# A cross-attention kernel: the first weight chunk in two transfers, six warming rounds, and four early reads of a few bytes

## The reference

```
q = x @ Wq + bq                      # 512 -> 512
k = ctx @ Wk + bk                    # 256 -> 512
v = ctx @ Wv + bv                    # 256 -> 512
w = softmax((q @ k^T) / sqrt(512), axis=tokens)   # over the 100 tokens, not over the context
y = w @ v + x
out = (y - mean(y)) * rsqrt(var(y) + 1e-6) * gamma + beta
```

## Time and profile before

| | |
|---|---|
| time, median of 3 executions | 142.33 us (142.27 to 143.05) |
| time of the profiled execution | 142.47 us |
| its span, first instruction to last | 140.7 us |
| busy: TensorE, VectorE, ScalarE, GpSimd | 134.4, 115.1, 79.7, 60.8 us |
| mean granted TensorE clock | 0.992 |

### The profile page before, as it was taken

How to read it: one execution, slowest core, us unless ns; L and a number is a source line. 1 busy time by engine, 2 the same in 40 slices (tenths; PEclk the granted TensorE clock), 3 DMA queues, 4 the chain that set the end, 5 groups by cost and what they waited for, 6 DMA issues and landing times.

```text
span 140.7 us, 2977 instructions
## 1 busy us (share of the span) xinstructions
PE 134.4 (96%) x1046; PEld 130.0 (92%) x1046; DVE 115.1 (82%) x224; ACT 79.7 (57%) x283; POOL 60.8 (43%) x61
## 2 busy tenths in 40 slices
PE   7999999999999999999999999999999999999940
PEld 7899999999998999999999999999999999998940
DVE  0689995996996779999999976878799976797983
ACT  4267098667276925567473829474746546386420
POOL 1000000037304581733839370629475643629791
PEclk9999999999999999999999999999999999999996
DMA  4999999985187595986978789697987987536314
GB/s 139 328 404 420 424 278 389 302 285 199 20 261 269 175 374 166 366 328 198 349 289 301 285 305 370 234 330 224 301 278 280 342 260 256 209 108 221 121 73 150
DMA packets 10814, 37.33 MB, mean 265 GB/s; under 512 B 1200, under 2 KB 1456, under 8 KB 10800
## 3 DMA queue, kind: packets, MB, share of 16 engines
q1 hardware_dynamic: 9424, 34.79, 71.6%
q10 hardware_dynamic: 1376, 2.36, 4.4%
HBM read 33.87 MB, written 3.28 MB: 264 GB/s over the span
## 4 chain that ended last, share of the span: by engine, by line
PE 89%; POOL 5%; issue 2%; ACT 1%; POOLq 0%; DVE 0%; DVEq 0%
PE ps_S L424 29%; PE ps_U L438 26%; PE ps_Y L459 10%; PE ps_U L397 6%; PE ps_Y L397 6%; POOL xT_in L979 3%; PE ps_Y L340 2%; POOL xT_in L967 2%; PE ps_S L345 1%; PE ps_w L447 1%; PE ps_U L504 1%; PE ps_c L412 1%; PE ps_S L351 1%; PE ps_U L351 1%; ACT xT_in L601 1%
## 5 line engine op out<-in xcount | busy, mean ns | idle before, releaser
L583 ACT ACTIVATE expo<-scores,negmax 121x100 f32<-121x100 f32 x96 | 35.0, 365 | 31.0 <-DVE negmax L754 30.9
L424 PE MATMUL ps_S<-G,ctxT_in 128*121 128x100 f32 (+1 forms) x384 | 43.4, 269 | 0.0
L424 PEld LDWEIGHTS ps_S<-G,ctxT_in 128*121 128x121 f32 (+1 forms) x384 | 42.1, 185 | 0.0
L438 PEld LDWEIGHTS ps_U<-prob,ctx_in 121*128 121x128 f32 x336 | 39.4, 192 | 0.9
L438 PE MATMUL ps_U<-prob,ctx_in 121*128 121x100 f32 x336 | 39.6, 274 | 0.0
L956 POOL TENSOR_TENSOR prob<-expo,rinv 121x600 f32<-121x600 f32 x16 | 19.2, 1202 | 30.4 <-DVE rinv L761 30.2
L967 POOL TENSOR_TENSOR xT_in<-x_in,xT_in 128x512 f32<-128x512 f32 (+1 forms) x13 | 17.1, 1315 | 19.8 <-issue 8.9
L750 DVE TENSOR_TENSOR scores<-ps_S,c_rows 121x600 f32<-121x600 f32 x16 | 12.5, 782 | 10.1 <-PE ps_S L424 7.4
L765 DVE TENSOR_REDUCE probsum<-prob 121x100 f32<-121x600 f32 x16 | 19.8, 1239 | 1.0 <-POOL prob L956 0.7
L583 ACT ACTIVATION_READ_ACCUMULATOR expo<-scores,negmax 121x1 f32 x96 | 17.9, 187 | 0.0
L972 POOL TENSOR_TENSOR rstd<-vareps,neg_half 128x1 f32<-128x1 f32 (+1 forms) x13 | 7.1, 549 | 23.3 <-DVE vareps L792 23.1
(11 more groups left out here) (120 smaller groups left out, 184.4 us busy)
## 6 DMA issues: line engine op xcount, KB each, us to landing
ctx_in<-ctx SPq DMA_DIRECT2D x16, 768.0 KB, 5.2
ctxT_in<-ctxT SPq DMA_DIRECT2D x16, 722.0 KB, 5.1
xT_in<-xT SPq DMA_DIRECT2D x8, 400.0 KB, 8.6
x_in<-x SPq DMA_DIRECT2D x12, 256.0 KB, 4.5
out<-xT_in ACTq DMA_DIRECT2D x8, 256.0 KB, 4.1
wqk<-Wqk SPq DMA_DIRECT2D x4, 388.0 KB, 4.6
out<-xT_in SPq DMA_DIRECT2D x3, 256.0 KB, 2.0
wv_in<-Wv SPq DMA_DIRECT2D x1, 512.0 KB, 16.3
```

What stands on the lines that cost most here:

```text
L424: last = nc.tensor.matmul(ps_scores(c)[0:rows(c), :], ctxT_in[:, q, l * M + c * MP:l * M + c * MP + rows(c)], G[:, l, bass.ds(b * T, T)], ...
L438: last = nc.tensor.matmul(ps_U[:, q, l * T:(l + 1) * T], ctx_in[0:rows(c), q, c, l * P:(l + 1) * P], prob[0:rows(c), q, c * T:(c + 1) * T] ...
L583: last = nc.scalar.activation(expo[0:MP, q, c * T:(c + 1) * T], scores[0:MP, q, c * T:(c + 1) * T], ACT.Exp, bias=negmax[0:MP, q, c:c + 1] ...
```

## The change

The first chunk comes in two transfers: first its columns 256 to 775 (half of Wq, with all of Wk and the biases), with a semaphore of its own, `first_w_in`; then columns 0 to 255, which complete `w_in[0]`. The blocks that go through TensorE in float32 are now the two whose columns come first, 2 and 3, and `split_columns` names the other two. TensorE and VectorE wait for `first_w_in` where they waited for `w_in[0]`; ScalarE and VectorE's last step of the chunk wait for `w_in[0]`. WARM is 6. At the very beginning, ScalarE issues four DMAs, each of one number from 16 rows, out of the third and the fourth weight chunk and out of the first half of x's first and of its second group; they land in `touched`, which nobody reads. SyncE waits for them at the end.

```diff
-        WARM = 7
+        WARM = 6
...
+        touched = sb("touched", [P, 4])
...
-            return slice(EC // 2 * P, E) if f == 0 else slice(0, E)
+            return slice(0, E // 2) if f == 0 else slice(0, E)
...
-            for c in range(EC):
+            sp.dma_start(wqk[:, 0, E // 2:], Wqk[0, :, E // 2:]).then_inc(first_w_in, 16)
+            sp.dma_start(wqk[:, 0, 0:E // 2], Wqk[0, :, 0:E // 2]).then_inc(w_in[0], 16)
+            for c in range(1, EC):
                 sp.dma_start(wqk[:, c, :], Wqk[c]).then_inc(w_in[c], 16)
...
+            for n in range(4):
+                sp.wait_ge(touch_done[n], 16)
             sp.wait_ge(out_stored[0], 16 * (NT - NT // 2 + 1))
...
-            pe.wait_ge(w_in[0], 16)
-            for e in range(EC // 2):
+            pe.wait_ge(first_w_in, 16)
+            for e in range(EC // 2, EC):
...
-                blocks = range(EC // 2, EC) if f == 0 else range(EC)
+                blocks = range(EC // 2) if f == 0 else range(EC)
...
+            for n, region in enumerate((Wqk[2], Wqk[3], xT[0, 0], xT[1, 0])):
+                act.dma_start(touched[0:16, n:n + 1], region[0:16, 0:1], allow_slow_non_contiguous=True).then_inc(touch_done[n], 16)
             act.wait_ge(consts_set, 1)
...
-                dve.wait_ge(w_in[c], 16)
+                dve.wait_ge(first_w_in if c == 0 else w_in[c], 16)
...
+                if c == 0:
+                    dve.wait_ge(w_in[0], 16)
```

More of the change, by code:

```diff
@@ L119, in xattn @@
         xT_loaded = [[sem(f"xT_loaded{g}_{h}") for h in range(2)] for g in range(NG)]
+        touch_done = [sem(f"touch_done{n}") for n in range(4)]
         wv_loaded = sem("wv_loaded")
@@ L128, in xattn @@
         onesr_set = sem("onesr_set")
+        first_w_in = sem("first_w_in")
         wqhi_set = sem("wqhi_set")
```

## The result

The changed kernel is slower: 143.06 us (median of 22 executions, 142.40 to 143.62) against 142.30 (22 executions, 141.63 to 143.05), ratio 1.0055, interval 1.004 to 1.0069. I had forecast 141.9, in a range of 141.4 to 142.7. Half of a per cent is passed on the side to which I had given 0.1.

A forecast was written before the change was run, and what follows sets the result against it. TensorE, working 134.4 of 140.7 us, was taken as the bound. An earlier start (0.17) plus the removed stand before chunk three (0.26) gave -0.43 us, so 142.33 becomes 141.9, range 141.4 to 142.7.

The forecast's parts named there:

- the side to which I had given 0.1: Whole kernel: slower by more than half a per cent, needing late `first_w_in` and the postponed level; chance 0.10.
- SyncE's additional issue: Start of the load stream: costs 0.45 us, delaying the issues of chunks three and four, but hidden.
- The split and the round: Program start: first transfer lands at 3.61, six rounds end about 3.53, TensorE starts 0.33 us earlier.
- the 0.17 us: TensorE's first chunk: half of its 0.33 us earlier start, left when the clock level changes.
- The reads: Early reads by ScalarE: remove 0 or all of chunk three's 1.39 us delay; all was taken.
- the hole: Slow stretch of the load stream at chunk three: 234 GB/s against 420 later, step 1.39 us too long.
- steady 0.26 us: TensorE's stand at 8.06 us, waiting for chunk three; forecast to go if the reads work.
- second rival: First chunk's load: the reads' first-access cost delays it; -0.1 to +0.25 us, 144.5 at most; chance 0.22.
- The waits at the end: Program end: SyncE's waits for the four reads cost nothing, since it waits for the last store anyhow.

The follow-up runs named there:

- e5: The kernel before with only the first chunk split in two transfers (seven rounds, no reads): 142.83 against 142.31 us, ratio 1.0041.
- e1: The changed kernel without the four early reads (split and six rounds stay): 142.98 against 142.57 us for the kernel before, ratio 1.0026.
- e4: The changed kernel with seven warming rounds instead of six: 143.54 against 142.57 us for the kernel before, ratio 1.0062.
- e16: The changed kernel, unaltered, profiled a second time: 143.09 us, a typical value.
- e3: The kernel before with six warming rounds instead of seven and nothing else: 143.0 against 142.57 us, ratio 1.0016 without the three longest.
- e6: The kernel before with four early reads, all from the first chunk: 142.73 against 142.31 us, ratio 1.0026.
- e12: The kernel before with one small transfer more on SyncE's queue, behind chunk four: 142.61 against 142.18 us, ratio 1.0016.
- e2: The kernel before with nothing added but the four early reads: 142.64 against 142.57 us, ratio 1.0002.
- e9: The kernel before with the four early reads counting on one semaphore, waited for once: 142.26 against 142.18 us, ratio 1.0005.
- e15: The kernel before, unaltered, profiled a second time: 141.73 us.
- e13: The changed kernel with its four reads on one semaphore: 142.77 against 142.35 us for the kernel before, ratio 1.0041.
- e7: The kernel before with one small transfer more on SyncE's queue, between chunks one and two: 143.26 against 142.31 us, ratio 1.0059.
- e10: The kernel before with chunks two and three joined in one transfer: 142.61 against 142.18 us, ratio 1.0041.
- e11: The kernel before with chunks three and four joined in one transfer: 142.72 against 142.18 us, ratio 1.0044.
- e8: The kernel before with chunks one and two joined in one transfer: 144.71 us in a single execution.

## Why the prediction was wrong

**The step that failed** is the one on SyncE's additional issue and the second transfer, priced at nothing ("Their turns in the stream come after 4.9 and 5.9. Hidden."). I looked only at the issue, and took the stream behind chunk one as unchanged, 0.98 us for each chunk. It isn't: with a second short transfer ahead of it, chunk two lands 1.6 to 2.4 us after chunk one, and TensorE stands until 0.80 us after that landing (0.77 us in the changed kernel's profile). Alone this is 0.41% or 0.58 us (e5); with six rounds 0.26%, 0.37 us (e1).

**The split and the round** were right up to TensorE's start: VectorE began on the first transfer at 3.60 (landing at 3.61 forecast), TensorE at 3.71 (3.72). But the 0.17 us that this should leave are lost again: a TensorE that waits for chunk two anyhow gains nothing by beginning earlier. The ratios of e5 and e1 (seven and six rounds, 0.58 and 0.37) and of e4 and the changed kernel (0.88 and 0.78) lean to the side of a gain, but the differences are within their intervals. The first projection at 10.77 in the changed kernel's first profile (10.7 forecast) is luck: it is the fastest of 22 executions, and the typical one of e16 has it at 11.36.

**The reads.** I took the end at which they remove 1.39 us of the hole, worth 0.26. The premise was weak: the hole at chunk three has no fixed size in the kernel before (ScalarE starts on it at 7.29 in one profile, at 6.11 in the next), and where it came without a split TensorE stood for it in one profile of four (the first one of before; in e3, e6 and e12 it was still busy with chunk two when chunk three was ready). So there was no steady 0.26 us to gain. Whether the reads take that hole away stays open: in both profiles with reads of later places and no split (e2, e9) it is gone, but in e15 too. Inside the span they are worth nothing that can be measured (e2: -0.13 us on the mean; e9: ratio 1.0005). My second rival, the reads pay in front, may be seen in e2 and e9 (chunk one at 4.28 and 4.50), but it isn't what made the changed kernel slow. The Trainium skill ("DMA: Bandwidth & Descriptors", Queues, rings and completion order) has every engine take turns between the queues; that agrees with chunk one's later landing in e2 and e9, but e6 had it at 3.85 with as many reads and e12 at 4.30 with none, so the profiles don't settle it.

**The waits at the end, "nothing".** The waits may be; the four semaphores or these waits cost 0.2 us outside the span (1.99 in the changed kernel, 2.00 to 2.08 in e4 and e6, 1.80 in e13, 1.73 in e9). I had looked only inside the span.

The sum as measured: the split, with reads on one semaphore and six rounds, 0.58 us (e13; e5, the split alone, has the same), and 0.2 for the semaphores. Together 0.78, the result's ratio of 0.55%. Without reads e1 has 0.37 in place of 0.58; that the reads add 0.2 behind a split is possible, but within the intervals.

**What stays open** is why a short transfer ahead makes rows of chunk two slow. Over 3.5 to 4.5 us, what the rows took beyond their even time adds up to 0.19 to 0.36 us for each DMA engine in the seven split profiles, and to 0.11 or less in all others (e7, whose slow rows come later, has 0.10). By place in the queue alone it can't be explained: third transfers have no hole in e10 and e11. Nor is it shown how e7 loses its time, or why e11, whose stream is ahead of that of before, is slower. No version of this study beats the kernel before; e2, e3, e9 and e12 can't be told from it.

## What to carry to other kernels

Cutting the first transfer to start earlier also changes the transfers behind it; follow the landing of the second and third, not only that of the first. Where a gain rests on one gap in one profile, look whether the gap is there in a second profile of the same kernel before building on it. Where a chunk's landing sets TensorE's next start, an earlier beginning only lengthens the wait. Four semaphores more, each with its wait, cost 0.2 us outside the span, which no view of the span shows: compare the time with the span.

## What the runs showed of the hardware

Transfers of 128 rows of 3104 bytes run at one in 0.98 us, but in the first 7 us there is mostly a hole that delays one of them by up to 1.5 us (e6: 2.46 us from chunk two to chunk three), besides the slow start, and its place depends on the transfers ahead. In the hole the DMA engines count as busy (share 0.88 at 234 GB/s); single rows of 0.122 us take up to 1.57. A transfer of 64 bytes, in second place on the queue, went with a chunk two 1.64 us behind chunk one and with 0.59% of time (e7). Of four kernels with two chunks in one transfer, three had no hole behind the first landing (e8, e10, e11; one profile each, and e8's stream began slowly). The 2.4 GHz level of TensorE came between about 4 and 6.9 us after the span's start over 17 profiles, at 5.4 and at about 4.7 in two of the same kernel, and after a pause of 1.6 us (3.96 to 5.53, e8) only at 9.4. Four semaphores with their waits cost about 0.2 us.
